# Value products of two key tiles in one run, every second slot, with four tiles of exponentials

## The chip, the cores and the metric

One core of a Trainium2 chip. The metric is device time in microseconds (us) of one launch. The engines have these names: PE is TensorE's matmuls, PEld its weight loads, DVE is VectorE, ACT is ScalarE, POOL is GpSimd, SP is SyncE, which issues the DMAs.

## What is computed

Two layers over a stream `x` of 8 batches x 100 tokens x 128. Each layer adds a gated cross-attention to a context of 1444 keys per batch, then a gated mixture of experts:

```
x = x + tanh(g_xattn[l]) * attention_l(layernorm(x), context)
x = x + tanh(g_ffn[l])   * experts_l(layernorm(x))
```

Attention has 16 heads of 8. Layer 0 masks keys; layer 1 multiplies the attention weights of each key with a sigmoid of its "energies". Layer 0's experts choose 8 of 64 by groups, layer 1's 2 of 8. Only the attention part is touched by the change, in both layers.

## The kernel before

Everything is written as one program for each engine, and the engines are tied by semaphores alone. The order on an engine is the order in the code.

**Tiling.** The 1444 keys of a batch are cut into 12 key tiles of 121 rows (the last has 113). The 16 heads are four groups (g = 0 to 3) of four heads; one score matmul gives a group's scores of a key tile: 121 keys x 400 (4 heads x 100 queries). The scores land in `ps`, which has two PSUM banks, used in turn. ACT takes each bank through the exponential into `probs` (L847), one instruction per group. `weigh` (L1177 to L1193) then multiplies the exponentials of a whole key tile with the values, 16 small matmuls that the trace shows as 32 records on PE (32 columns of weights each), accumulating in the bank `po`.

**Slots.** A batch is 12 slots, one for each key tile t (L1232 to L1253). The PE's order in a slot is written out by hand. In what follows s0 to s3 are the score matmuls of the four groups, each in layer 0 with a mask matmul behind it (L1167, L1171), W is one `weigh` run, and Q ("quad") is four matmuls into `pm` (L1137) with which the row maxima of a later batch are found:

- layer 0: s0, s1, Q, W, s2, s3, then `beside`
- layer 1: s0, s1, W, s2, Q, s3, then `beside`

W in slot t is that of the tile before, t-1 (in slot 0 the last tile of the batch before). `beside` (L1215) puts other work behind s3: the turning and projection of the batch before in slots 1 to 3, the key projections of a later batch in slots 4 to 6 (L1102), the value projections of the next one in slots 7 to 9 (L1115). Batch 7, the last, has no Q, nor have the last two slots of batch 6.

**Waits.** A score matmul n waits until ACT has emptied its bank, which is exponential n-2 (L1165). The exponential waits for its scores and, as `probs` has two tiles, for W of the tile two before (L846). W waits for all four exponentials of its tile (L1179). Q goes in two halves of two banks each; its first half waits for the first half of the quad before to be taken by DVE, its second half for the second (L1133 to L1136). In layer 0 a quad's kind is "pair" (DVE L423, two instructions) or "third" (L427, four); each third quad is a third. In layer 1 it is two reductions (L420).

**ACT's order** in a slot: exponentials 0, 1, (the copy of `po` of the batch before in slot 0), 2, 3, and behind them in slots 4 to 6 the copy of the key projection (L857), in slots 7 to 9 that of the value projection (L871).

**Others that wait for W.** SP stacks the keys of batch b (L1393) and POOL makes its queries and values (L694, L706) when all W of batch b-2 are done.

**Buffers.** `wb` (four tiles of 128 x 800) holds routing weights during the experts' stage alone.

Of the kernel before, what the change touches and what calls it, by code (L numbers as in the profile page):

```python
# [32 lines left out]
ACT = mybir.ActivationFunctionType  # L33
AX = mybir.AxisListType.X

B, S, D = 8, 100, 128
NK = 1444
KEY_TILE = 121
KEY_TILES = -(-NK // KEY_TILE)
# [3 lines left out]
HQ = H * S  # L43
GQ = J * S
# [6 lines left out]
TOK = B * S  # L51
# [13 lines left out]
RING = 4  # L65
# [28 lines left out]


MASK_ROWS = 31


PARTS = {"a": (0, 6), "b": (6, 8)}
# [29 lines left out]
def flamingo(nc, a, out, scratch):  # L129
    with ExitStack() as ctx:  # L130
        def sb(name, shape, dt=F32):
            return ctx.enter_context(nc.sbuf_tensor(name, shape, dt))
# [66 lines left out]
        rowmax = sb("rowmax", [100, 128])  # L199
        mrow = sb("mrow", [H, S], F32R)  # L200
        junk = sb("junk", [100, 2, 2, MAX_W], BF16)
        probs = [sb(f"probs{i}", [KEY_TILE, HQ]) for i in range(2)]
        oraw = sb("oraw", [128, GQ])
        rden = sb("rden", [100, H])
        onorm = sb("onorm", [100, D])
# [20 lines left out]
            return v  # L226

        wts = [sb(f"wts{i}", [128, 3, 128]) for i in range(RING)]
        wb = [sb(f"wb{i}", [128, TOK]) for i in range(RING)]
        sg = [over(tmpf, v * HALF, [128, HALF]) for v in range(2)]  # L230
        tu = [over(vaug[0], TOK + v * HALF, [128, HALF]) for v in range(2)]
        hw = [over(tmpf, 2 * HALF, [128, HALF]), over(t2, 0, [128, HALF])]
# [556 lines left out]
        def _(act):  # L789
            n = [0]  # L790
# [47 lines left out]
            def attention(l):  # L838
                s = A[l]

                def exp_group(b, t, g):
                    r, n = rows_of(t), (b * KEY_TILES + t) * G + g
                    act.wait_ge(s["scores_ready"], n + 1)

                    if b * KEY_TILES + t >= 2:
                        act.wait_ge(s["pv_done"], b * KEY_TILES + (t - 1))  # L846
                    nc.scalar.activation(probs[t % 2][0:r, g * GQ:(g + 1) * GQ], ps[0:r, n % 2, 0:GQ], ACT.Exp,  # L847
                                         scale=SCALE).then_inc(s["probs_ready"], 1)

                def k_high(b, c):  # L850
                    lo, w = CHUNKS[c]
                    act.wait_ge(s["kproj_done"], b * 3 + (c + 1))
                    if b >= 2 and c == 0:

                        act.wait_ge(s["chunk_ready"], (b - 1) * 2 * QUADS)
                        act.wait_ge(s["kstack_in"][b % 2], landed(b - 2, b % 2, 2, 192))
                    nc.scalar.activation(khi[b % 2][:, lo:lo + w], pc[:, 0:w], ACT.Identity, bias=bk[l][:, 0:1])\  # L857
                        .then_inc(s["khi_ready"], 1)

                def max_row(b):  # L860

                    act.wait_ge(s["maxrow_ready"], b + 1)
                    if b >= 1:
                        act.wait_ge(s["mrow_in"][(b - 1) % 2], landed(b - 1, (b - 1) % 2, 2, 16))
                    nc.scalar.activation(mrow[:], pc[0:H, 0:S], ACT.Identity, scale=-1.0).then_inc(s["mrow_ready"], 1)

                def v_raw(b, c):
                    act.wait_ge(s["vproj_done"], b * 3 + (c + 1))

                    act.wait_ge(s["v_written"], (b * 3 + c - 1) * (1, 2)[l])  # L870
                    nc.scalar.copy(vraw[(c + b) % 2][:].rearrange("p t n -> p (t n)"), pc[0:KEY_TILE, :])\  # L871
                        .then_inc(s["vraw_ready"], 1)

                def outputs(b):

                    act.wait_ge(s["pv_done"], b * KEY_TILES + KEY_TILES)
                    if b >= 1:
                        act.wait_ge(s["onorm_ready"], b)
                    nc.scalar.copy(oraw[:], po[:, 0:GQ]).then_inc(s["oraw_ready"], 1)

                def slots(b):

                    for t in range(KEY_TILES):
                        exp_group(b, t, 0)
                        exp_group(b, t, 1)
                        if b >= 1 and t == 0:
                            outputs(b - 1)
                        exp_group(b, t, 2)
                        if t == ROW_SLOT and b < B - 1:
                            max_row(b + 1)  # L890
                        exp_group(b, t, 3)
                        if b < B - 2 and 0 <= t - K_SLOT < 3:
                            k_high(b + 2, t - K_SLOT)
                        if b < B - 1 and 0 <= t - V_SLOT < V_CHUNKS:
                            v_raw(b + 1, t - V_SLOT)
                        if b == B - 1:

                            if t == 0:
                                root(2 * l + 1, "a")
                            if t == TURN_SLOT:  # L900
                                part_turned(2 * l + 1, 0)
                                part_turned(2 * l + 1, 1)
                            if t == LOGITS_SLOT and l == 0:
                                router0("a")

                for c in range(len(CHUNKS)):
                    k_high(1, c)
                max_row(0)
                slots(0)
                if l == 0:  # L910
                    act.wait_ge(dve_done, marks["energy"])
                    step(nc.scalar.activation(egate[:], egate[:], ACT.Exp, scale=-1.0), "energy_exp")
                for b in range(1, B):
                    slots(b)
                outputs(B - 1)
# [112 lines left out]
        def _(pe):  # L1028
            n = [0]
# [58 lines left out]
            def attention(l):  # L1088
                s = A[l]
# [87 lines left out]
                def weigh(b, t):  # L1177
                    r = rows_of(t)
                    pe.wait_ge(s["probs_ready"], (b * KEY_TILES + t) * G + G)  # L1179
                    if t == 0:  # L1180

                        pe.wait_ge(s["v_written"], (b * 3 + 3) * (1, 2)[l])
                        if b >= 1:
                            pe.wait_ge(s["oraw_ready"], b)
                    for g in range(G):
                        for j in range(J):
                            h = J * g + j
                            mm = nc.tensor.matmul(po[32 * j:32 * j + 32, g * S:(g + 1) * S],  # L1188
                                                  vaug[b % 2][0:r, t, 9 * h:9 * h + 32],
                                                  probs[t % 2][0:r, h * S:(h + 1) * S],  # L1190
                                                  start=(t == 0 and g == 0), stop=(t == KEY_TILES - 1),
                                                  tile_position=(0, 32 * j), skip_group_check=True)
                    mm.then_inc(s["pv_done"], 1)  # L1193
# [38 lines left out]
                def slots(b):  # L1232

                    for t in range(KEY_TILES):
                        if t < ROW_SLOT:
                            quad = (b + 1, QUADS_AHEAD + t) if b < B - 1 else None
                        else:
                            quad = (b + 2, t - ROW_SLOT) if b < B - 2 else None
                        scores(b, t, 0)
                        scores(b, t, 1)  # L1240
                        if quad and l == 0:
                            max_quad(*quad)
                        if t >= 1:
                            weigh(b, t - 1)
                        elif b >= 1:
                            weigh(b - 1, KEY_TILES - 1)
                        scores(b, t, 2)
                        if t == ROW_SLOT and b < B - 1:
                            max_rows(b + 1)
                        if quad and l == 1:  # L1250
                            max_quad(*quad)
                        scores(b, t, 3)
                        beside(b, t)  # L1253
# [7 lines left out]
                    max_quad(1, k)  # L1261
                for b in range(B):
                    slots(b)
                weigh(B - 1, KEY_TILES - 1)
                turn_out(B - 1)
                turn_back(B - 1)
# [109 lines left out]
        def _(sp):  # L1376
# [93 lines left out]
            def experts(l):  # L1470
# [10 lines left out]
                def spread(u, slot):  # L1481

                    if not (isinstance(u, int) and u < RING):

                        sp.wait_ge(m["weighted"], u * 2 - (2 * RING - 2))
                    if l == 0:
                        for i in range(2):
                            sp.dma_start(wb[slot][64 * i:64 * i + 64, :],
                                         scratch[0][bass.ds(u * 2 + i, 1), :].broadcast_to([64, TOK]))\
                                .then_inc(m["wb_in"][slot], 16)  # L1490
                    else:
                        sp.dma_start(wb[slot][:], scratch[1][bass.ds(u * 16, 16), :].unsqueeze(1)
                                     .broadcast_to([16, 8, TOK])).then_inc(m["wb_in"][slot], 16)

                for u in range(RING):
# [98 lines left out]
```

## Time and profile before

| | us |
|---|---|
| median of 3 runs | 1073.51 |
| lowest, highest | 1071.07, 1082.74 |
| profiled execution, first to last instruction (span) | 1069.7 |
| PE busy | 912.3 |
| DVE busy | 749.6 |
| ACT busy | 579.7 |

No time of the profiled execution besides its span is listed; what lies around the span is read from the runs: the lowest is 1.4 above it, the median 3.8. In the rows below a timeline line reads: start, duration (us), engine, line of the code, operation, output <- input, shape, count; in brackets the idle time of that engine just before, and what ended it. Matmul ends are modelled, so starts are the safer reading; the start of a weight load (PEld) is where a matmul enters PE.

### The profile page before, as it was taken

The page shows a single profiled execution, that of the slowest core. Times are in us where ns is not written, and L with a number is a line of the kernel's source. Part 1 is how long each engine was busy: PE and PEld are TensorE (multiplying, and loading weights), DVE is VectorE, ACT ScalarE, POOL GpSimd, SP SyncE. Part 2 cuts the span into 40 slices and gives each one's busy share as a digit, 9 for nine tenths or more (in the row PEclk, how much of TensorE's full clock was granted, in tenths as well). Part 3 has the DMA queues.
Part 4 walks back from the last instruction along what each step waited for, and adds up shares of the span by engine and source line. Part 5 has one row for each costly group of instructions (what it writes and reads, how often), then busy time and mean ns, then how long its engine had stood idle before and what let it go on. Part 6 is the DMA issues. An engine that isn't in the chain of part 4 may idle for free.

```text
span 1069.7 us, 24592 instructions
## 1 busy us (share of the span) xinstructions
PE 912.3 (85%) x9812; PEld 631.5 (59%) x9812; DVE 749.6 (70%) x1420; ACT 579.7 (54%) x1214; POOL 309.6 (29%) x276
## 2 busy tenths in 40 slices
PE   4569899999999987699997679999999998842996
PEld 2126566666666654588885236566666656532885
DVE  6676677777676727589997966877877874042996
ACT  2305465665655575256664135777767767621664
POOL 2600202112112100167673501242234212002764
PEclk9558899999999998599998657999999998865999
DMA  6670404034032110376551620431342231016651
GB/s 152 113 160 2 101 13 113 30 85 112 30 85 47 40 32 2 89 213 170 163 152 25 159 58 1 113 95 48 86 112 57 58 85 32 1 18 133 166 160 54
DMA packets 49007, 90.01 MB, mean 84 GB/s; under 512 B 21816, under 2 KB 32252, under 8 KB 48892
## 3 DMA queue, kind: packets, MB, share of 16 engines
q1 hardware_dynamic: 48892, 88.44, 34.4%
q8 instruction: 77, 1.26, 0.5%
q14 instruction: 38, 0.31, 0.1%
HBM read 47.32 MB, written 1.75 MB: 46 GB/s over the span
## 4 chain that ended last, share of the span: by engine, by line
PE 59%; DVE 14%; ACT 9%; POOL 6%; issue 5%; DMA 4%; SPq 2%; POOLq 0%; DVEq 0%; ACTq 0%
PE ps L1167 20%; PE po L1188 15%; PE pm L1137 9%; POOL tmpf L771 6%; ACT probs L847 4%; PE ps L1171 4%; PE pc L1102 4%; PE pc L1115 3%; DVE vaug L533 3%; DVE qsel L524 3%; ACT qsel L941 3%; DMA routing<-vaug 2%; DVE mx_part L420 2%; DVE junk L423 2%; DVE junk L427 1%
## 5 line engine op out<-in xcount | busy, mean ns | idle before, releaser
L847 ACT ACTIVATE probs<-ps 121x400 f32<-121x400 f32 (+1 forms) x768 | 356.8, 503 | 211.7 <-PE ps L1171 126.0
L1167 PE MATMUL ps<-qst,kst 128*121 128x400 f32 (+3 forms) x768 | 318.9, 461 | 30.1 <-ACT probs L847 29.0
L420 DVE TENSOR_REDUCE mx_part<-pm 100x2 f32<-100x964 f32 x192 | 213.7, 1158 | 65.6 <-PE pm L1137 65.5
L1167 PEld LDWEIGHTS ps<-qst,kst 128*121 128x121 f32 (+3 forms) x768 | 141.9, 189 | 146.4 <-ACT probs L847 91.3
L1276 PE MATMUL pm<-qsel,qst 128*128 128x400 f32 x660 | 158.3, 363 | 39.8 <-DVE qsel L524 35.9
L423 DVE CUSTOM_DVE_ANT_0 junk<-pm,negq 100x964 bf16<-100x964 f32 x128 | 143.5, 1158 | 55.6 <-PE pm L1137 55.5
L1188 PE MATMUL po<-probs,vaug 121*32 121x100 f32 x6144 | 179.3, 259 | 1.5 <-ACT probs L847 1.5
L1188 PEld LDWEIGHTS po<-probs,vaug 121*32 121x32 f32 x6144 | 135.2, 113 | 55.1 <-ACT probs L847 32.0
L1137 PE MATMUL pm<-khi,qbd 32*100 32x482 f32 x768 | 129.5, 490 | 37.4 <-DVE mx_part L420 12.9
L1276 PEld LDWEIGHTS pm<-qsel,qst 128*128 128x128 f32 x660 | 122.2, 195 | 58.8 <-DVE qsel L524 57.9
L771 POOL TENSOR_TENSOR tmpf<-vaug,wb 128x400 f32<-128x400 f32 x55 | 68.4, 1243 | 220.3 <-DMA wb<-routing 160.6
L1171 PE MATMUL ps<-negT,ident_b 121*121 121x276 bf16 (+1 forms) x384 | 111.5, 290 | 0.0
L1137 PEld LDWEIGHTS pm<-khi,qbd 32*100 32x100 f32 x768 | 46.8, 174 | 104.0 <-issue 34.7
L524 DVE TENSOR_TENSOR qsel<-tmpf,qsel 128x400 fp32r<-128x400 f32 x55 | 61.9, 1126 | 49.2 <-ACT qsel L941 49.2
L712 POOL TENSOR_TENSOR vaug<-vraw,bv 121x512 f32<-121x512 f32 x24 | 31.8, 1327 | 220.6 <-ACT vraw L871 212.0
L427 DVE CUSTOM_DVE_ANT_0 junk<-pm,negq 100x482 bf16<-100x482 f32 x128 | 76.6, 655 | 21.9 <-PE pm L1137 21.9
L1276 PE MATMUL ps<-qsel,qst 128*128 128x400 f32 x330 | 83.3, 363 | 1.1 <-DVE qst L516 1.1
L712 POOL TENSOR_TENSOR vraw<-vraw,bv 121x512 f32<-121x512 f32 x24 | 30.7, 1277 | 173.4 <-ACT vraw L871 173.4
L941 ACT CAST qsel<-tmpf 128x400 fp32r<-128x400 f32 x55 | 29.0, 527 | 88.0 <-POOL tmpf L771 88.0
L696 POOL TENSOR_TENSOR qst<-qsel,head_mask 96x400 fp32r<-96x400 f32 x64 | 52.6, 851 | 76.6 <-PE po L1188 67.9
L771 POOL TENSOR_TENSOR t<-vaug,wb 128x400 f32<-128x400 f32 x55 | 73.0, 1327 | 0.0
L1276 PEld LDWEIGHTS ps<-qsel,qst 128*128 128x128 f32 x330 | 64.4, 200 | 1.7 <-DVE qsel L568 1.4
(179 smaller groups left out, 893.3 us busy)
## 6 DMA issues: line engine op xcount, KB each, us to landing
kst<-khi SPq DMA_DIRECT2D x128, 180.5 KB, 4.0
wb<-routing SPq DMA_DIRECT2D x66, 200.0 KB, 3.7
ctxT<-in_ctxT SPq DMA_DIRECT2D x16, 722.0 KB, 4.2
kst<-klo SPq DMA_DIRECT2D x64, 180.5 KB, 4.0
wts<-in_experts SPq DMA_DIRECT2D x55, 192.0 KB, 3.7
wb<-routing SPq DMA_DIRECT2D x22, 400.0 KB, 4.1
qsel<-qhi SPq DMA_DIRECT2D x16, 100.0 KB, 2.4
kst<-kst SPq DMA_DIRECT2D x7, 180.5 KB, 3.4
```

What stands on the lines that cost most here:

```text
L420: ins = nc.vector.tensor_reduce(parts[:, 2 * i:2 * i + 2, j, x], bank, AX, ALU.max)
L423: ins = nc.vector.tensor_tensor_reduce(junk[:, i], bank, mask, 1.0, -3e38, ALU.add, ALU.max, parts[:, x + i, j, 0:1])
L427: ins = nc.vector.tensor_tensor_reduce(junk[:, i, g % 2, :], pm[0:S, g, 0:MAX_W], negq[:, NK - MAX_W:NK], 1.0, -3e38, ALU.add, ALU.max, pa ...
L524: nc.vector.tensor_tensor(h_lo[v], hw[v], h_hi[v], ALU.subtract).then_inc(m["h_low"], 1)
L712: nc.gpsimd.tensor_tensor(raw4 if l else dst, raw4, bias, ALU.add).then_inc(s["v_written"], 1)
L771: nc.gpsimd.tensor_tensor(hw[v], tu[v], wb[slot][:, v * HALF:(v + 1) * HALF], ALU.mult).then_inc(m["weighted"], 1)
L847: nc.scalar.activation(probs[t % 2][0:r, g * GQ:(g + 1) * GQ], ps[0:r, n % 2, 0:GQ], ACT.Exp, scale=SCALE).then_inc(s["probs_ready"], 1)
L1137: mm = nc.tensor.matmul(pm[0:S, bank, 0:MAX_W], qbd[b % 2][rows, j * S:(j + 1) * S], khi[b % 2][rows, lo:lo + MAX_W], start=True, stop=Tru ...
L1167: mm = nc.tensor.matmul(ps[0:r, n % 2, 0:GQ], kst[b % 2][0:rows, g, t * KEY_TILE:t * KEY_TILE + r], qst[b % 2][0:rows, g * GQ:(g + 1) * GQ ...
L1171: mm = nc.tensor.matmul(ps[0:r, n % 2, 0:GQ].rearrange("p (j q) -> p j q", q=S)[:, :, MASK_ROWS:S], ident_b[0:r, 0:r], negT[0:r, t, MASK_R ...
L1188: mm = nc.tensor.matmul(po[32 * j:32 * j + 32, g * S:(g + 1) * S], vaug[b % 2][0:r, t, 9 * h:9 * h + 32], probs[t % 2][0:r, h * S:(h + 1) ...
L1276: mm = nc.tensor.matmul(dst, w, x, start=(alone and k == 0), stop=(alone and k == 2), skip_group_check=not alone)
```

## The change

`probs` becomes a ring of four tiles; the two new tiles lie over the memory of `wb`, which becomes one tensor, `shared`. The exponential of tile t waits for W of tile t-4. In odd slots there is no W. In even slots t there are two W, of tiles t-2 and t-1, one behind the other at the place where one stood (in slot 0 those of the last two tiles of the batch before). Behind the last slot of batch 7 stand two W. The number of matmuls, exponentials and transfers stays as it was.

```diff
+PROBS = 4
...
-        probs = [sb(f"probs{i}", [KEY_TILE, HQ]) for i in range(2)]
...
-        wb = [sb(f"wb{i}", [128, TOK]) for i in range(RING)]
+        shared = sb("shared", [128, RING * TOK])
+        wb = [shared[:, i * TOK:(i + 1) * TOK] for i in range(RING)]
+        probs = [sb(f"probs{i}", [KEY_TILE, HQ]) for i in range(2)] + [over(shared, i * HQ, [KEY_TILE, HQ]) for i in range(2)]
...
-                    if b * KEY_TILES + t >= 2:
-                        act.wait_ge(s["pv_done"], b * KEY_TILES + (t - 1))
-                    nc.scalar.activation(probs[t % 2][0:r, g * GQ:(g + 1) * GQ], ps[0:r, n % 2, 0:GQ], ACT.Exp,
+                    if b * KEY_TILES + t >= PROBS:
+                        act.wait_ge(s["pv_done"], b * KEY_TILES + (t - PROBS + 1))
+                    nc.scalar.activation(probs[t % PROBS][0:r, g * GQ:(g + 1) * GQ], ps[0:r, n % 2, 0:GQ], ACT.Exp,
...
-                                                  probs[t % 2][0:r, h * S:(h + 1) * S],
+                                                  probs[t % PROBS][0:r, h * S:(h + 1) * S],
...
-                        if t >= 1:
+                        if t >= 1 and t % 2 == 0:
+                            weigh(b, t - 2)
                             weigh(b, t - 1)
-                        elif b >= 1:
+                        elif t == 0 and b >= 1:
+                            weigh(b - 1, KEY_TILES - 2)
                             weigh(b - 1, KEY_TILES - 1)
...
+                weigh(B - 1, KEY_TILES - 2)
                 weigh(B - 1, KEY_TILES - 1)
...
-                        sp.dma_start(wb[slot][:], scratch[1][bass.ds(u * 16, 16), :].unsqueeze(1)
+                        sp.dma_start(wb[slot], scratch[1][bass.ds(u * 16, 16), :].unsqueeze(1)
```

## Rows read from the trace of the kernel before

**Rows 1.** The page: busy time by engine, and the chain's shares.
```profile
PE 912.3 (85%) x9812; PEld 631.5 (59%) x9812; DVE 749.6 (70%) x1420; ACT 579.7 (54%) x1214; POOL 309.6 (29%) x276
...
PE 59%; DVE 14%; ACT 9%; POOL 6%; issue 5%; DMA 4%; SPq 2%; POOLq 0%; DVEq 0%; ACTq 0%
```

**Rows 2.** Stretches of 50 us, layer 1: busy time by engine, granted clock.
```profile
core 0: us, PE busy (x) PEld busy (x) DVE busy (x) ACT busy (x) POOL busy (x), PEclk, DMA share, GB/s
...
600.00:650.00 50.00, 39.17 (x223) 17.74 (x225) 35.84 (x36) 13.12 (x26) 7.38 (x9) 0.50 0.30 68
...
750.00:800.00 50.00, 47.79 (x691) 30.19 (x691) 39.53 (x45) 35.04 (x74) 15.13 (x16) 1.00 0.47 105
```

**Rows 3.** Timeline, layer 0, batch 3: slot 1's s2 up to slot 2's s2.
```profile
216.84 0.18 PEld L1167 LDWEIGHTS ps<-qst,kst 128*121 128x121 f32 x1 [0.15 <-issue]
...
218.00 0.18 PEld L1167 LDWEIGHTS ps<-qst,kst 128*121 128x121 f32 x1
...
218.29 0.08 DVE L423 DVE_READ_ACCUMULATOR2_ANT mx_part<- 100x1 f32 x1
...
218.39 0.18 PEld L1167 LDWEIGHTS ps<-qst,kst 128*121 128x121 f32 x1 [0.16 <-ACT probs L847]
...
218.60 0.90 ACT L847 ACTIVATE probs<-ps 121x400 f32<-121x400 f32 x2 [0.26 <-PE ps L1171]
...
218.89 0.25 PEld L1137 LDWEIGHTS pm<-khi,qbd 32*100 32x100 f32 x4 [0.27 <-issue]
...
219.50 0.67 PEld L1188 LDWEIGHTS po<-probs,vaug 121*32 121x32 f32 x32 [0.36 <-ACT probs L847]
...
220.32 0.18 PEld L1167 LDWEIGHTS ps<-qst,kst 128*121 128x121 f32 x1 [0.15 <-issue]
```

**Rows 4.** Timeline, same batch: DVE's end of a quad, and the next quad.
```profile
225.20 0.08 DVE L427 DVE_READ_ACCUMULATOR2_ANT mx_part<- 100x1 f32 x1
...
225.65 0.68 PE L1137 MATMUL pm<-khi,qbd 32*100 32x482 f32 x4
...
232.29 0.08 DVE L423 DVE_READ_ACCUMULATOR2_ANT mx_part<- 100x1 f32 x1
...
232.95 0.47 PE L1137 MATMUL pm<-khi,qbd 32*100 32x482 f32 x4
```

**Rows 5.** Timeline, layer 1, a batch's slot 0 from s2 to slot 1's quad.
```profile
749.79 0.18 PEld L1167 LDWEIGHTS ps<-qst,kst 97*121 97x121 f32 x1 [0.15 <-ACT probs L847]
...
750.16 0.17 PEld L1137 LDWEIGHTS pm<-khi,qbd 32*100 32x100 f32 x4 [0.19 <-DVE mx_part L420]
...
750.66 2.23 DVE L420 TENSOR_REDUCE mx_part<-pm 100x2 f32<-100x964 f32 x2 [0.76 <-PE pm L1137]
751.03 1.54 ACT L847 ACTIVATE probs<-ps 121x400 f32<-121x400 f32 x3 [0.21 <-PE ps L1167]
...
751.58 0.18 PEld L1167 LDWEIGHTS ps<-qst,kst 97*121 97x121 f32 x1 [0.53 <-ACT probs L847]
...
751.96 0.67 PEld L1188 LDWEIGHTS po<-probs,vaug 121*32 121x32 f32 x32 [0.20 <-ACT probs L847]
...
752.78 0.18 PEld L1167 LDWEIGHTS ps<-qst,kst 97*121 97x121 f32 x1 [0.15 <-ACT probs L847]
...
753.15 0.17 PEld L1137 LDWEIGHTS pm<-khi,qbd 32*100 32x100 f32 x4 [0.19 <-issue]
```

**Rows 6.** Timeline, layer 1, slot 5, behind a key projection: exponentials, then s2.
```profile
764.42 1.53 ACT L847 ACTIVATE probs<-ps 121x400 f32<-121x400 f32 x3
...
764.96 0.44 PE L1167 MATMUL ps<-qst,kst 97*121 97x400 f32 x1
```

**Rows 7.** Timeline, layer 1, batch 7: s0 and s1 of a slot, then s2 and s3.
```profile
925.94 0.84 PE L1167 MATMUL ps<-qst,kst 97*121 97x400 f32 x2 [0.41 <-ACT probs L847]
...
927.53 0.63 PE L1167 MATMUL ps<-qst,kst 97*121 97x400 f32 x2
```

**Rows 8.** The chain in order of time, layer 1, batch 0: W of two slots.
```profile
634.90 1.49 PE po L1188 x32
639.57 1.49 PE po L1188 x32
```

## The prediction

> **What bounds the kernel now.** I read the page first. PE is busy for 85% of the span and carries 59% of the chain that ended last; DVE and ACT have 14% and 9% [rows 1]. That asks for less PE time, and the change seems to give it, since two W in one run enter and leave W's form of matmul once. But a busy share is an average. So I went on to the timeline of one slot in each layer, for which wait ends last at each step.
>
> Layer 0 [rows 3]: from s2 (216.84) to the next slot's s1 (218.39) are 1.55 us in which s1 waits for ACT. From s1 to the quad 0.50, quad to W 0.61, W to s2 0.82: PE alone. Together 3.48, the slot. Layer 1 [rows 5]: s2 (749.79) to s1 (751.58) 1.79, again ended by ACT; s1 to W 0.38, W to s2 0.82; together 2.99. So the stretch from s1 to s2, where W stands, is PE's, and while W runs ACT makes exponentials 0 and 1, for which s2 and s3 must wait. The reader is to see that W covers ACT's latency, and that DVE's quad ends only shortly before the next quad begins (218.29 + 0.08 = 218.37 against 218.89 [rows 3]).
>
> **The change part by part.**
>
> *Counts.* Each layer has 96 W. 48 leave odd slots. 47 come as the second run in an even slot (slots 2 to 10 of eight batches are 40, slot 0 of batches 1 to 7 are 7), and one more stands behind the last slot, where PE waits for exponentials anyway: I count it as nothing (0.67 at most).
>
> *The second run.* No row shows two W in a row. One W's 32 weight loads take 0.67, and s2 starts 0.15 behind the last [rows 3, 5]. A second W of the same form should add 0.67; at most 0.82, if the way out is paid again; a gain is excluded, as 32 pairs of instructions must be issued. I take 0.67, since inside W the 32 follow without a gap: 47 x 0.67 = 31.5 us per layer.
>
> *Odd slots, layer 0.* Without W, s2 follows the quad. Rows show quad to W at 0.61; quad to s2 I take as the same, as both change the form of the matmul. So 0.82 goes, if s2's bank is free: exponential 0 starts 0.60 behind s0 and lasts some 0.45 (two take 0.90), to 219.05; s2 would enter at 219.50. It is free. I take 0.81 a slot. What is late next is DVE. The next quad comes 0.81 earlier, and its second half needs the whole quad before. From slot 1: DVE done 218.37, some 0.04 to PE, quad due at 218.89 - 0.81 = 218.08: a stall of 0.33 [rows 3]. Behind a third quad: 225.28 + 0.04 against 225.65 - 0.81, 0.48; behind the extra DVE work and the longer slots 5 to 9: 232.37 + 0.04 against 232.95 - 0.81, 0.27 [rows 4]. With slots 1 and 11 at 0.33, slot 3 at 0.48, slots 5, 7, 9 at 0.27 it is 1.95 a batch, bounds 0 and 6 x 0.48 = 2.9. Even slots have their long run behind the quad, so DVE catches up there.
> Layer 0: six odd slots save 4.9 in each of batches 0 to 6, 34; batch 7 has no quad, s2 waits for exponential 0 and saves about 0.6 (end 219.05, so 0.70 behind s1 in place of 0.50 + 0.82 [rows 3]), 3.6; stalls are 6 x 1.95 and about 1.5 in batch 6, 13.2. So 31.5 + 13.2 - 37.6 = +7.
>
> *Odd slots, layer 1.* Here W stands straight between s1 and s2, and ACT decides once it is gone. Exponentials 3, 0, 1 start at 751.03 and run on (pitch about 0.46, one 0.50 long); exponential 0 ends at 751.99, so s2 can enter at 752.04 instead of 752.78: 0.74 saved [rows 5]. But the quad behind s2 moves to 752.41, and DVE finishes the quad before at 750.66 + 2.23 = 752.89; with 0.04 the second half is released 0.52 late. 0.22 is left. In slots 5, 7 and 9 ACT first copies a projection: exponential 0 runs from 764.42 to 764.92 and s2 enters at 764.96 already now [rows 6]: nothing is saved there, and W in these slots was free. So slots 1, 3, 11 give 0.22 each, 0.66 a batch, 4.0 in batches 0 to 5; batch 6 (no key projections, no quad in its last slots) 1.6; batch 7: s0 at 925.94, exponential 0 ends 0.47 + 0.50 later, s2 enters near 926.95 instead of 927.53 [rows 7], 0.58 x 6 = 3.5. Layer 1: 31.5 - 9.1 = +22. Bounds: 0.74 saved in all 21 odd slots of batches 0 to 6 that have no copy and no stall (about 11 us less) and nothing saved anywhere (9 us more).
>
> *Ring, waits, buffers.* The exponential's wait is now for W of tile t-4, which has run at least a slot earlier: it never ends last, but it also brings no earlier start, since `ps` still has two banks and an exponential needs its scores. Behind the wait in ACT's queue stand only later exponentials. SP's key stacks and POOL's queries and values for the next batch come free 0.67 later, in slot 0, and are due a batch later (some 35 us): nothing. SP issues the same transfers into the same bytes of `wb` in the experts' stage, when no exponential is live: nothing.
>
> *The clock.* In 600 to 650 us PE was granted 0.50, its 1.2 GHz, and a slot of layer 1 took 4.67 us (634.90 to 639.57) [rows 2, 8]; at 1.00 it takes 2.99. If the rise comes a slot earlier or later through the new rhythm, that is 1.7 us each time. I take 0, with 8 either way (five slots).
>
> *Sum:* 7 + 22 = +29 on the span of 1069.7, so 1098.7. The runs lie 1.4 (lowest) to 3.8 (median) above the span; I add 2: 1101 us, against the median of 1073.5.
>
> *A rule weighed.* Rows show gaps of 0.15 behind W and 0.20 before it in layer 1 [rows 5]. The Trainium skill, "TensorEngine Tiling (Array Packing)", Key Properties, states that a change of tiling mode drains TensorE. The trace agrees as far as there is a gap at each such change; by the rule alone each joined pair of runs would save PE these gaps, which is the first rival below.
>
> **The rivals.**
>
> *PE alone decides (faster).* If s2 didn't wait for ACT nor the quad for DVE, an odd slot would save 0.81 in layer 0, and in layer 1 1.20 less the 0.37 between s2 and the quad, 0.83 [rows 5]; less 0.67 that is 0.14 and 0.16 a pair, 47 x 0.30 = 14: 1058 us. For it: PE's share. Against it: both layers' s1 already wait for ACT, and two banks leave ACT no lead. It decides if exponential 0 ended before s1 + 0.37 in layer 1; the rows have 0.41 without the quad's wait, so it would also need DVE's quad 0.5 us shorter.
>
> *DVE doesn't stall (within 1%).* If the quad's second half has its banks in time, 13 go in layer 0 and about 11 in layer 1: +5, 1077 us. For it: matmul ends and releases are inferred. Against it: quad and DVE starts are measured, and 2.23 + 0.50 exceeds 752.41 - 750.16.
>
> *The second run pays its entry again (slower still).* 94 x 0.15 = 14 more: 1115 us.
>
> *The clock.* If batch 0 of layer 1 stays at 1.2 GHz, or batch 7 falls lower for longer, up to 8 more: 1109 us; sooner up: 1093.
>
> **How the numbers follow.** The forecast 0.62 (its own range 1090 to 1109, with the clock at its bounds), PE alone 0.10, no stall 0.15, entry paid again 0.08, more clock loss 0.05. A measurement of this kernel tells about 1% (10.7 us) from no change. Faster by over 1%: the first rival, 0.10. Within 1%: the second, and a tail of the forecast, 0.17. Slower: 0.73. The range of 1076 to 1113 leaves out the first rival and half of the third, and holds the bounds of the unknown costs but for their extremes.
>
> **What would show it.** Right: in the new timeline W comes as a run of 64 with weight loads of about 1.34 us; odd slots of layer 1 about 2.8 us with s2 ended by ACT and the quad by DVE, even ones about 3.7; odd slots of layer 0 about 2.7, even ones about 4.4 with the quad ended by DVE; PE's idle time before L1167 and L1137 grown, its busy time about as before. Wrong: odd slots in layer 1 near 2.1 us; a quad that never waits for DVE; or more than 0.1 us between the two runs.

## The result, and the profile after

The changed kernel takes 1140.57 us (median of 4 runs, 1135.45 to 1144.25) against 1072.29 for the kernel before (4 runs beside it, 1068.88 to 1082.74): a ratio on record of 1.0595, with an interval of 1.0515 to 1.0676; the two medians alone give 1.0637, so a difference between runs that is given in us is good to some 5 us. The sign was as forecast, the size was not: 1101 was predicted, and 1113 was the upper end. The profiled execution took 1141.88 us, its span is 1140.1.

Line numbers in the new kernel are 4 higher up to W (L1141 is the quad, L1171 the scores, L1192 W, L851 the exponential). The two new tiles of exponentials appear as `shared`. First the page of the changed kernel, the rows that answer to [rows 1], with the granted clock in 40 slices:

```profile
PE 962.0 (84%) x9812; PEld 672.2 (59%) x9812; DVE 749.1 (66%) x1420; ACT 578.1 (51%) x1214; POOL 309.8 (27%) x276
...
PEclk9559899999999996799996598986868988775999
...
PE 55%; DVE 18%; ACT 9%; issue 6%; POOL 5%; DMA 4%; SPq 2%; POOLq 0%; ACTq 0%; DVEq 0%
```

The clock line of the kernel before, from its page:

```profile
PEclk9558899999999998599998657999999998865999
```

PE does the same 9812 instructions and is busy 50 us longer. DVE's share of the chain grew from 14% to 18%, as a quad that waits for DVE would have it. But the largest difference is in the clock line. Before, after the dip of layer 1's first batch (6, 5, 7), there are eight slices at 9. After, the dip (6, 5) is followed by 9, 8, 9, 8, 6, 8, 6, 8, 9, 8, 8. The next view says it in numbers; it is that of 50 us stretches of the changed kernel (columns as in [rows 2]):

```profile
750.00:800.00 50.00, 45.46 (x527) 29.84 (x527) 31.34 (x35) 28.20 (x61) 11.06 (x11) 0.80 0.26 61
800.00:850.00 50.00, 46.46 (x521) 30.18 (x519) 30.32 (x34) 26.61 (x57) 11.05 (x11) 0.73 0.26 61
```

In the middle of layer 1 the granted clock is 0.80 and 0.73, where it was 1.00 [rows 2], and PE gets through 527 matmuls in 50 us instead of 691. PE's busy share hardly shows it (45.46 against 47.79 us), since the same matmuls are busy for longer at 1.2 GHz (W's run of 64 further down: 1.36 us of weight loads at 2.4 GHz, 2.54 at 1.2).

To see where the time went I take the length of each batch, from one copy of `po` (ACT, slot 0) to the next, in the timelines:

| us a batch | layer 0, batches 1 to 7 | sum | layer 1, batches 1 to 7 | sum |
|---|---|---|---|---|
| before | 46.3, 42.3 x4, 40.2, 37.9 | 293.7 | 37.2 x5, 36.0, 37.7 | 259.6 |
| after | 47.9, 43.5 x4, 41.2, 39.8 | 302.9 | 44.9, 45.1, 47.8, 50.0, 44.9, 44.2, 41.2 | 318.0 |

The copies that bound a batch of layer 1, before and after (in the changed kernel the longest batch):

```profile
712.71 0.49 ACT L879 COPY oraw<-po 128x400 f32<-128x400 f32 x1 [0.35 <-PE po L1188]
749.92 0.49 ACT L879 COPY oraw<-po 128x400 f32<-128x400 f32 x1 [0.35 <-PE po L1188]
```

```profile
825.00 0.49 ACT L883 COPY oraw<-po 128x400 f32<-128x400 f32 x1 [2.35 <-PE po L1192]
875.01 0.49 ACT L883 COPY oraw<-po 128x400 f32<-128x400 f32 x1 [2.25 <-PE po L1192]
```

Layer 0 grew evenly, by 1.2 in each of its batches 2 to 5 and 9.2 in all. Layer 1 grew by 58.4, and unevenly, though its batches 1 to 5 do identical work: that is no sum of waits, which would be the same in each.

**Layer 0** in the timeline of the changed kernel, an odd slot's s1 up to the next slot's s2, answers to [rows 3]:

```profile
219.83 0.18 PEld L1171 LDWEIGHTS ps<-qst,kst 128*121 128x121 f32 x1 [0.16 <-ACT probs L851]
...
220.33 0.25 PEld L1141 LDWEIGHTS pm<-khi,qbd 32*100 32x100 f32 x4 [0.26 <-issue]
220.95 0.18 PEld L1171 LDWEIGHTS ps<-qst,kst 128*121 128x121 f32 x1 [0.37 <-ACT probs L851]
...
222.50 0.18 PEld L1171 LDWEIGHTS ps<-qst,kst 128*121 128x121 f32 x1 [0.16 <-ACT probs L851]
...
223.00 0.16 PEld L1141 LDWEIGHTS pm<-khi,qbd 32*100 32x100 f32 x1 [0.27 <-issue]
223.34 0.25 PEld L1141 LDWEIGHTS pm<-khi,qbd 32*100 32x100 f32 x3 [0.18 <-DVE mx_part L427]
223.95 1.36 PEld L1192 LDWEIGHTS po<-probs,vaug 121*32 121x32 f32 x64 [0.36 <-ACT shared L851]
225.46 0.18 PEld L1171 LDWEIGHTS ps<-qst,kst 128*121 128x121 f32 x1 [0.15 <-issue]
```

The odd slot is 222.50 - 219.83 = 2.67 long (2.7 was forecast). In the even one W comes as one run of 64, 1.36 of weight loads, and W to s2 is 1.51 where it was 0.82: a second W costs 0.69. The quad waits for DVE: W enters 0.95 behind the quad's first load (223.00 to 223.95), 0.34 later than the 0.61 of before. A pair of slots thus pays 0.69 + 0.34 - 0.81 = 0.22, six pairs 1.3 a batch.

**Layer 1** in the same view, slots 0 to 2 of batch 1, answers to [rows 5]:

```profile
685.59 1.36 PEld L1192 LDWEIGHTS po<-shared,vaug 121*32 121x32 f32 x64 [0.19 <-ACT probs L851]
687.10 0.18 PEld L1171 LDWEIGHTS ps<-qst,kst 97*121 97x121 f32 x1 [0.15 <-issue]
...
688.90 0.18 PEld L1171 LDWEIGHTS ps<-qst,kst 97*121 97x121 f32 x1 [0.53 <-ACT probs L851]
689.30 0.18 PEld L1171 LDWEIGHTS ps<-qst,kst 97*121 97x121 f32 x1 [0.21 <-ACT probs L851]
689.67 0.16 PEld L1141 LDWEIGHTS pm<-khi,qbd 32*100 32x100 f32 x2 [0.19 <-issue]
690.26 0.17 PEld L1141 LDWEIGHTS pm<-khi,qbd 32*100 32x100 f32 x2 [0.43 <-DVE mx_part L424]
...
692.99 2.54 PEld L1192 LDWEIGHTS po<-probs,vaug 121*32 121x32 f32 x64 [0.47 <-issue]
```

Up to 690.26 every step is as forecast: s2 to s1 1.80 as before, s1 to s2 0.40 (forecast 0.46), and the quad's second half comes 0.59 behind its first, released by DVE (forecast 0.52). Then the next run of W takes 2.54 for the same 64 loads. The windows of 1 us at this place, same columns, show why:

```profile
689.00:690.00 1.00, 1.00 (x4) 0.43 (x4) 1.00 (x2) 0.86 (x3) 1.00 (x2) 1.00 0.91 205
690.00:691.00 1.00, 0.86 (x5) 0.33 (x3) 1.00 (x2) 0.28 (x1) 1.00 (x2) 0.68 0.96 208
691.00:692.00 1.00, 1.00 (x5) 0.86 (x6) 1.00 (x2) 0.43 (x1) 0.38 (x1) 0.50 0.94 191
```

The clock fell from 2.4 to 1.2 GHz (0.50) at about 690.4 (the microsecond from 690 has 0.68), in the slot that no longer has a W. Read in fine windows, batches 1 to 6 of layer 1 hold 13 such falls with some 92 us at 1.2 GHz in all; the kernel before has none in these batches. The ten of batches 1 to 5 all begin behind the W of slot 10 and ahead of that of slot 4, and end before the W of slot 6; from slot 4 to slot 9, where `beside` has the key and value projections, none begins. The three of batch 6, which has no key projections, come in slots 3 to 7. Each of the 13 begins between two runs of W. At 1.2 GHz a run of 64 to s2 takes 2.82 (692.99 to 695.81) instead of 1.51.

The waits of the changed kernel, engine, line, what it waited for, then total, times, longest:

```profile
DVE mx_part L424 <- PE pm L1141: 118.4, 68, 4.4
...
PEld pm L1141 <- DVE mx_part L424: 32.2, 38, 3.3
```

and of the kernel before:

```profile
DVE mx_part L420 <- PE pm L1137: 65.5, 86, 2.4
...
PEld pm L1137 <- DVE mx_part L420: 28.8, 39, 3.3
```

DVE waits 53 us more for layer 1's quads. So DVE is not what holds layer 1: over most of a batch it is PE, which is slow, that is late.

### The profile page after: what moved, and what is told of

Same layout as the page of the kernel before. It is cut to its first block, busy times and chain, and to the rows that moved or that the text cites. A ratio compares the mean times of both kernels' runs of the same rounds, so it can differ in the third digit from the quotient of the medians.

```text
span 1140.1 us, 24576 instructions
## 1 busy us (share of the span) xinstructions
PE 962.0 (84%) x9812; PEld 672.2 (59%) x9812; DVE 749.1 (66%) x1420; ACT 578.1 (51%) x1214; POOL 309.8 (27%) x276
## 4 chain that ended last, share of the span: by engine, by line
PE 55%; DVE 18%; ACT 9%; issue 6%; POOL 5%; DMA 4%; SPq 2%; POOLq 0%; ACTq 0%; DVEq 0%
PE ps L1171 16%; PE po L1192 15%; PE pm L1141 9%; DVE mx_part L424 5%; POOL tmpf L775 5%; PE pc L1106 4%; PE ps L1175 3%; PE pc L1119 3%; DVE qsel L528 2%; DVE vaug L537 2%; ACT shared L851 2%; ACT qsel L945 2%; DVE junk L431 2%; ACT probs L851 2%; DMA routing<-vaug 2%
## 5 line engine op out<-in xcount | busy, mean ns | idle before, releaser
L1171 PE MATMUL ps<-qst,kst 128*121 128x400 f32 (+3 forms) x768 | 330.6, 476 | 48.0 <-ACT probs L851 25.0
L1171 PEld LDWEIGHTS ps<-qst,kst 128*121 128x121 f32 (+3 forms) x768 | 147.2, 197 | 185.2 <-ACT probs L851 69.3
L851 ACT ACTIVATE shared<-ps 121x400 f32<-121x400 f32 (+1 forms) x384 | 177.7, 502 | 136.0 <-PE ps L1175 66.1
L851 ACT ACTIVATE probs<-ps 121x400 f32<-121x400 f32 x384 | 178.7, 504 | 126.3 <-PE ps L1175 61.9
L1141 PE MATMUL pm<-khi,qbd 32*100 32x482 f32 x768 | 152.5, 511 | 40.8 <-DVE mx_part L424 14.2
L775 POOL TENSOR_TENSOR tmpf<-vaug,shared 128x400 f32<-128x400 f32 x55 | 68.5, 1245 | 228.9 <-DMA shared<-routing 167.1
L1141 PEld LDWEIGHTS pm<-khi,qbd 32*100 32x100 f32 x768 | 56.2, 179 | 119.9 <-issue 44.1
L1192 PE MATMUL po<-shared,vaug 121*32 121x100 f32 (+1 forms) x3072 | 91.1, 280 | 0.0
L1192 PE MATMUL po<-probs,vaug 121*32 121x100 f32 x3072 | 88.3, 275 | 0.0
L1192 PEld LDWEIGHTS po<-shared,vaug 121*32 121x32 f32 (+1 forms) x3072 | 79.4, 125 | 14.4 <-issue 8.1
L1192 PEld LDWEIGHTS po<-probs,vaug 121*32 121x32 f32 x3072 | 77.0, 123 | 15.5 <-issue 8.0
```

What stands on the lines that cost most here:

```text
L775: nc.gpsimd.tensor_tensor(hw[v], tu[v], wb[slot][:, v * HALF:(v + 1) * HALF], ALU.mult).then_inc(m["weighted"], 1)
L851: nc.scalar.activation(probs[t % PROBS][0:r, g * GQ:(g + 1) * GQ], ps[0:r, n % 2, 0:GQ], ACT.Exp, scale=SCALE).then_inc(s["probs_ready"], 1)
L1141: mm = nc.tensor.matmul(pm[0:S, bank, 0:MAX_W], qbd[b % 2][rows, j * S:(j + 1) * S], khi[b % 2][rows, lo:lo + MAX_W], start=True, stop=Tru ...
L1171: mm = nc.tensor.matmul(ps[0:r, n % 2, 0:GQ], kst[b % 2][0:rows, g, t * KEY_TILE:t * KEY_TILE + r], qst[b % 2][0:rows, g * GQ:(g + 1) * GQ ...
```

## The experiments

Two theories of the falls stood against each other. A: the odd slots have lost work and gained waits (for ACT behind s1, for DVE in the quad), and PE, so thinned, falls in clock; the expectations below name the waits alone. R: the run of 64 small matmuls does it by itself. All ratios are against the kernel before on the same chip.

**The ring alone (ring_only).** The order of before, with four tiles of exponentials in the new places:

```diff
-if t >= 1 and t % 2 == 0:
-    weigh(b, t - 2)
+if t >= 1:
     weigh(b, t - 1)
-elif t == 0 and b >= 1:
-    weigh(b - 1, KEY_TILES - 2)
+elif b >= 1:
     weigh(b - 1, KEY_TILES - 1)
...
-weigh(B - 1, KEY_TILES - 2)
```

> The ring of four tiles and the shared memory, with one W in each slot as before. Both theories: the ring's wait never ends last and the place of the tiles costs nothing, so the time of before, 1072 us within 5, low clock in layer 1 only in batches 0 and 7. If the place of the two new tiles or the wait costs something, it shows here as more than 5 us.

1069.23 us, ratio 0.9969 (0.9941 to 0.9997). The ring, its waits and the shared memory cost nothing, and bring next to nothing. Layer 1 ran at full clock:

```profile
750.00:800.00 50.00, 47.80 (x710) 30.24 (x702) 39.87 (x45) 34.75 (x74) 15.16 (x16) 1.00 0.47 105
```

**Pairs in one layer (pairs_l0, pairs_l1).** The order of after where `l == 0` (or `l == 1`), that of before in the other layer:

```diff
-if t >= 1 and t % 2 == 0:
-    weigh(b, t - 2)
-    weigh(b, t - 1)
+if l == 0:
+    if t >= 1 and t % 2 == 0:
+        weigh(b, t - 2)
+        weigh(b, t - 1)
...
+elif t >= 1:
+    weigh(b, t - 1)
```

> Two W in even slots in layer 0 alone, single W in layer 1. Forecast by the prediction's sum for layer 0: 7 us more than before, 1079 us; layer 1 as before, with its clock at 2.4 GHz in batches 1 to 6. If the loss were spread evenly over the layers it would be 1106 us.

1080.24 us, ratio 1.0062 (1.0036 to 1.0087): 6.7 us, as forecast. Its layer 0 took 300.9 in seven batches, 7.2 over before; its layer 1 the 259.6 of before.

> Two W in even slots in layer 1 alone, single W in layer 0. If layer 1 holds 22 us of waits and some 35 us of low clock: 1130 us, with stretches of 1.2 GHz in batches 1 to 6. If layer 0 holds half of the loss: 1106 us.

1137.13 us, ratio 1.0565 (1.0488 to 1.0642). By the ratios some 61 of the changed kernel's 64 us are layer 1's (by the medians 63 of 68), 7 more than expected, and they come without the other layer's change:

```profile
800.00:850.00 50.00, 45.46 (x529) 29.70 (x527) 30.81 (x34) 28.13 (x60) 12.28 (x12) 0.80 0.26 61
```

**The quad later (late_quad).** The changed kernel, with layer 1's quad behind s3 in odd slots, so that it comes later and waits less for DVE:

```diff
-if quad and l == 1:
+if quad and l == 1 and t % 2 == 0:
     max_quad(*quad)
 scores(b, t, 3)
+if quad and l == 1 and t % 2 == 1:
+    max_quad(*quad)
```

> The changed kernel with the quad of layer 1's odd slots behind s3, so that DVE has some 0.6 us more to finish the quad before. Theory A (the waits in the odd slots leave PE so idle that its clock falls): the wait for DVE goes, some 10 us, and the clock falls in fewer stretches: 1095 to 1115 us. Theory R (the run of 64 small matmuls itself lets the clock fall, the waits don't matter for it): the 10 us go but the low stretches stay: 1125 to 1132 us.

1111.67 us, ratio 1.0356 (1.0301 to 1.0411), with the same runs of 64. Batches 1 to 5 of layer 1 are 41.0 to 41.9 long where they were 44.9 to 50.0, and little more than one fall of 3.4 us a batch is left in them; batch 6 has several and is 43.0 long.

```profile
750.00:800.00 50.00, 45.41 (x672) 30.13 (x673) 35.78 (x39) 31.94 (x69) 16.43 (x16) 0.97 0.27 63
```

That is on A's side. PE's busy time is that of the changed kernel (45.41 against 45.46), with 672 matmuls in place of 527: a busy share does not tell the two apart.

**Half the products (half_products).** The changed kernel without the second W: the products of even key tiles are left out, so even slots have one run of 32 and odd slots none (the semaphore counts are adapted).

```diff
...
 if t >= 1 and t % 2 == 0:
-    weigh(b, t - 2)
     weigh(b, t - 1)
 elif t == 0 and b >= 1:
-    weigh(b - 1, KEY_TILES - 2)
     weigh(b - 1, KEY_TILES - 1)
...
-weigh(B - 1, KEY_TILES - 2)
```

> The changed order with only the second W of each pair: odd slots have none, even slots one, so no run of 64 is left; the products of the even key tiles are left out. The waits in the odd slots stay. By the prediction's sum layer 0 loses 24 us and layer 1 9 us against the kernel before. Theory A (the waits let the clock fall): stretches of 1.2 GHz in layer 1's batches 1 to 6 as in the changed kernel, some 30 us: 1060 to 1075 us. Theory R (the runs of 64 let it fall): no such stretches, 1035 to 1045 us.

1093.61 us, ratio 1.0201 (1.0135 to 1.0268). With 96 W less this kernel is slower than the one before. Both missed the size (A said 1060 to 1075, R 1035 to 1045), but R failed: no run of 64 is left, and the clock was low for longer than in the changed kernel.

```profile
750.00:800.00 50.00, 45.89 (x385) 27.78 (x384) 35.36 (x41) 31.20 (x66) 12.19 (x13) 0.77 0.42 96
```

Layer 0, which keeps its clock, gained: 39.4 a batch against 42.3. Layer 1 lost, 40.5 to 51.9 a batch against 37.2. The same saving makes the one layer faster and the other slower, since in layer 1 the clock falls.

**Each W twice (each_twice).** The kernel before, with every W run a second time in its own slot (numerator and denominator both double):

```diff
-for g in range(G):
+for again, g in [(k, g) for k in range(2) for g in range(G)]:
...
-    start=(t == 0 and g == 0), stop=(t == KEY_TILES - 1),
+    start=(t == 0 and g == 0 and again == 0), stop=(t == KEY_TILES - 1 and again == 1),
```

> The kernel before with each W issued twice in its slot (numerator and denominator are both doubled): a run of 64 in every slot of both layers and no odd slot without W. 192 second runs of 0.69 us: 132 us. Theory A: no new waits, the clock stays at 2.4 GHz in layer 1's batches 1 to 6, 1200 to 1210 us. Theory R: the clock falls in most slots of layer 1, over 1235 us.

1185.02 us (a single run; 1069.98 for the kernel before), 15 under A's range and 50 under R's bound. This is a run of 64 in every slot, and from 702.6 to behind the last batch the clock stays up. The window of 50 us, one run in the timeline, and the page's clock line:

```profile
750.00:800.00 50.00, 48.56 (x1017) 34.40 (x1020) 33.03 (x37) 29.15 (x62) 11.07 (x11) 1.00 0.27 62
```

```profile
704.60 1.36 PEld L1188 LDWEIGHTS po<-probs,vaug 121*32 121x32 f32 x64 [0.19 <-ACT probs L847]
```

```profile
PEclk8559999999999999689998569999999999985899
```

Runs of 64 do not bring the clock down by themselves: R failed a second time. A batch grew by 8.3 in layer 0 (42.3 to 50.6) and 8.2 in layer 1 (37.2 to 45.4), 12 times 0.69: the price of a second run, with no other wait in it. A's range was 15 too high: it charged all 192 runs in full, but batch 7 of layer 1, for one, grew by 3.4 alone (41.1 against 37.7), as it has none of the 13.7 us at 1.2 GHz that the kernel before has there.

**Idle matmuls in odd slots (filled, filled_three).** The changed kernel, with two matmuls of zeros added to `po` before s2 and again before the quad, in odd slots of layer 1:

```diff
+def filler(b, t):
...
+    for k in range(2):
+        nc.tensor.matmul(po[:, 0:GQ], zero_b[:, 0:128], zero_b[:, 0:GQ], start=False, stop=False,
+                         skip_group_check=True)
...
+if l == 1 and t % 2 == 1:
+    filler(b, t)
...
 scores(b, t, 2)
...
 if quad and l == 1:
+    if t % 2 == 1:
+        filler(b, t)
     max_quad(*quad)
```

> The changed kernel with idle work on PE in layer 1's odd slots: two matmuls of zeros (128 x 400, added to the accumulators) ahead of s2 and two ahead of the quad, where PE waits for ACT and for DVE anyway. The waits end when they did. Theory A: PE's clock stays at 2.4 GHz in batches 1 to 6, some 30 us go: 1100 to 1112 us. Theory R: the low stretches stay, 1130 to 1145 us.

1106.54 us, ratio 1.0334 (1.0263 to 1.0405), in A's range. PE does more work and the kernel is 34 us faster than the changed one: no fall in batches 1 to 6 (in the page's clock line, behind the dip of batch 0 stand ten slices at 9).

```profile
750.00:800.00 50.00, 47.05 (x649) 29.97 (x649) 34.69 (x37) 32.10 (x68) 14.60 (x14) 1.00 0.26 61
```

```profile
PEclk9558899999999988599998579999999999875999
```

Batches 1 to 5 are 41.8 long, 4.6 over before, where 3.4 was forecast. In slots 5, 7 and 9 the idle matmuls stand in PE's way (the runs of W in slots 6 and 8 are 7.42 apart, 7.06 in the changed kernel), so the next kernel has them in slots 1, 3 and 11 alone.

```diff
-if t > 1 or b >= 1:
+if (t > 1 or b >= 1) and t in (1, 3, 11):
```

> As the filled kernel, but with the idle matmuls in slots 1, 3 and 11 alone, where PE waits for ACT and DVE; in slots 5, 7 and 9 of the filled kernel the two ahead of the quad stood in no wait and cost 0.36 us each. Theory A: the clock stays at 2.4 GHz in batches 1 to 6 and what is left is the prediction's sum without the clock, 1.1 us a batch of layer 1 less than the filled kernel: 1097 to 1101 us. If the projections' slots needed the idle work too, low stretches come back: over 1106 us.

1104.05 us, ratio 1.0297 (1.0247 to 1.0348), 3 over what was expected. Batches 1 to 5 are 40.7 long, without a fall: 3.5 over before. The runs of W in slots 0, 2 and 4 of a batch stand 6.47 and 6.48 apart:

```profile
680.71 1.36 PEld L1192 LDWEIGHTS po<-shared,vaug 121*32 121x32 f32 x64 [0.20 <-ACT probs L851]
687.18 1.36 PEld L1192 LDWEIGHTS po<-probs,vaug 121*32 121x32 f32 x64 [0.20 <-issue]
693.66 1.36 PEld L1192 LDWEIGHTS po<-shared,vaug 121*32 121x32 f32 x64 [0.19 <-ACT probs L851]
```

Two slots of before are 2 x 2.99 = 5.98, so a pair costs 0.49; 0.67 - 0.22 = 0.45 was forecast. More than the 3 us are in batches 6 and 7 (42.1 and 42.4), where the clock falls from 904.3 on; `filled`, with idle matmuls in all odd slots, has 39.0 and 38.6 there.

**Both remedies (late_filled).** The later quad, with idle matmuls before s2 and before s3 in odd slots of layer 1:

```diff
+if l == 1 and t % 2 == 1:
+    filler(b, t)
 scores(b, t, 2)
...
-if quad and l == 1:
+if quad and l == 1 and t % 2 == 0:
     max_quad(*quad)
+if l == 1 and t % 2 == 1:
+    filler(b, t)
 scores(b, t, 3)
+if quad and l == 1 and t % 2 == 1:
+    max_quad(*quad)
```

> Late quad and idle matmuls together: the changed kernel with layer 1's odd quads behind s3, two matmuls of zeros ahead of s2 and two ahead of s3 in odd slots. Theory A: no wait for DVE and no low clock in batches 1 to 6. What is left is the second W (31 us a layer) against what odd slots save with ACT alone as their limit: layer 0's 7 us and in layer 1 31.5 less about 20, so 1085 to 1098 us. If the odd slots of layer 1 were held by something else than DVE and ACT, no gain over the two single edits: 1105 us or more.

1093.25 us, ratio 1.0218 (1.0184 to 1.0252), in the range of A. In odd slots the quad is no longer split by a wait, its four weight loads come together, and the clock holds in batches 1 to 6:

```profile
689.95 0.17 PEld L1141 LDWEIGHTS pm<-khi,qbd 32*100 32x100 f32 x4 [0.24 <-DVE mx_part L424]
```

```profile
750.00:800.00 50.00, 46.71 (x656) 29.55 (x659) 35.84 (x39) 33.46 (x72) 15.69 (x15) 1.00 0.31 76
```

It is the best version with pairs in both layers that was tried, and it is still slower than the kernel before: batches 1 to 5 of layer 1 take 40.1 to 40.4 against 37.2, idle matmuls included. With the 7.2 that pairs_l0 loses in layer 0, this shows that the pairs lose without the clock too.

**Idle matmuls in the kernel before (warm).** Its clock is low in batch 0 of layer 1 [rows 2, 8]. In both layers, matmuls of zeros were put behind the quads that open the attention (3 behind each of batch 0's, 8 behind each of batch 1's), and 8 behind W in slot 1 of batch 7, into banks that are written anew afterwards:

```diff
+def warm(bank, count):
+    for k in range(count):
+        nc.tensor.matmul(bank, zero_b[:, 0:128], zero_b[:, 0:512], start=True, stop=True,
+                         skip_group_check=True)
...
...
 max_quad(0, k)
+warm(ps[:, 0, :], 3)
...
```

> The kernel before with idle matmuls (zeros, into banks that are free then) where PE waits long: three behind each opening quad, eight behind each of the last two, eight in batch 7 where ACT loads its tables. If the low clock in batch 0 and batch 7 comes from those waits, batch 0 of layer 1 saves some 11 us, layer 0 some 3, batch 7 some 4: 1052 to 1062 us. If it has another cause: 1070 to 1080 us.

1060.49 us, ratio 0.9896 (0.9842 to 0.9949): in the range of the first case, and faster than both kernels by work that computes nothing. Batch 7 of layer 1 is 34.6 long where it was 37.7. The stretch that [rows 2] shows at 0.50 is at 0.90:

```profile
600.00:650.00 50.00, 43.11 (x343) 19.14 (x341) 40.68 (x40) 17.29 (x34) 7.38 (x9) 0.90 0.29 67
```

## Why the prediction was right or wrong, point by point

*The second run, 0.67.* Right: 0.69 in both layers, and no entry is paid again; that rival fell. The rule that was weighed is worth little here: in layer 0 a pair saves PE 0.81 in the odd slot and costs 0.69 in the even one, so the joined run spares 0.12, near the gap of 0.15 behind W, and DVE's stall of 0.34 takes more than that.

*Layer 0, +7.* Right: 7.2 in pairs_l0, 9.2 in the profile of the changed kernel (in batches 2 to 5 both have 43.5 a batch; they differ in batches 1 and 7). The odd slot and DVE's stall came out to within 0.03.

*Layer 1's waits, 4.02 - 0.66, about 3.4 a batch.* Right: 3.5 in batches 1 to 5 of filled_three, which keep the clock. Slots 5, 7 and 9 saved nothing, as said: the runs of slots 6 and 8 are 671.89 - 664.83 = 7.06 apart at full clock, and before the change the W of these slots stood 773.69 - 767.29 = 6.40 apart; the difference, 0.66, is the second W alone. The rows, changed kernel and kernel before:

```profile
664.83 1.36 PEld L1192 LDWEIGHTS po<-probs,vaug 121*32 121x32 f32 x64 [0.27 <-issue]
671.89 1.36 PEld L1192 LDWEIGHTS po<-shared,vaug 121*32 121x32 f32 x64 [0.26 <-issue]
```

```profile
767.29 0.67 PEld L1188 LDWEIGHTS po<-probs,vaug 121*32 121x32 f32 x32 [0.27 <-issue]
773.69 0.67 PEld L1188 LDWEIGHTS po<-probs,vaug 121*32 121x32 f32 x32 [0.27 <-issue]
```

The sum of these terms (1101) is near filled_three (1104). That it comes so near in all is in part luck: the falls of batches 6 and 7 add some 7 us to filled_three (against `filled`), and the dip in its batch 0, shorter than that of the kernel before (below), takes some off.

*The rivals on the faster side.* "PE alone" needed odd slots of layer 1 without waits; the rows above show both. "DVE doesn't stall" is refuted by the quad rows of both layers.

*The clock.* This is the step that failed: "I take 0, with 8 either way (five slots)". It cost some 32 to 36 us: the changed kernel and filled_three differ by idle matmuls alone, by 36.5 in the medians (1140.57 and 1104.05) and by 0.030 in the ratios (1.0595 and 1.0297), which is 32. Batches 1 to 5 of layer 1 hold 232.6 - 203.5 = 29.1 of it, for some 78 us at 1.2 GHz. The two profiles are 4.9 apart at slot 0 of batch 1 already (its W at 685.59 against 680.71), but 2.3 of that stand at the layer's first W (647.23 against 644.93), ahead of the first idle matmul, where the two programs are still the same; the other 2.6 lie in batch 0, whose dip ends at 659.6 in the one and at 648.3 in the other. Measured against the kernel before, the change did not prolong that dip: its last stretch at 1.2 GHz is 61.4 long before (594.5 to 656.0), 51.2 after (608.4 to 659.6) and 44.4 in filled_three. The forecast, and its rival "the clock" as well, asked only how long the dips that were already there would last. It did not ask whether an odd slot without W would make new ones. Of the signs that the prediction named for its being right, one failed with it: PE's busy time, "about as before", rose by 49.7. The trace of before had a hint, though not a clean one: its second dip, 901.7 to 915.4, lies in batch 7, the only batch with neither quads nor projections, where a slot holds least for PE. But it begins in the one long wait of that batch, 2.29 us in which ACT loads tables, and `warm`, with idle matmuls in that wait, has 3.4 us at 1.2 GHz in batch 7 instead of 13.7:

```profile
902.19 0.67 PEld L1167 LDWEIGHTS ps<-qst,kst 97*121 97x121 f32 x2 [2.29 <-ACT probs L847]
```

*What brings it down* is shown as far as this. Batches 1 to 6 of layer 1 hold 0 us at 1.2 GHz in the kernel before and some 92 in the changed one. Taking W out of a slot and leaving it out altogether (half_products) brings more, some 149; making the quad wait less (late_quad) brings less, some 34; idle matmuls in all odd slots bring it to 0 (filled, late_filled), in slots 1, 3 and 11 to some 10, all in batch 6 (filled_three); a W more in every slot, none taken out, has 0 (each_twice). What the runs do not separate is how much of it is missing work and how much waiting, as an emptied slot has both. The Trainium skill, "TensorE: Matmul & The Clock Gate", "A second HAM failure mode: psum-queue depth-cycling", tells of a kernel whose TensorE idles so often for short moments between groups of matmuls that its clock swings between the two levels. The trace agrees as far as the clock swings 13 times, with gaps of 0.19 to 0.53 in the rows of layer 1 above; but gaps of that size stand in [rows 5] too, where no fall came. Taken as a rival, this rule would have moved the forecast the right way. Why filled_three falls again in batches 6 and 7 stays open, and so does a kernel with `warm` and pairs together, which was not tried.

## What to carry to other kernels

Before work is taken out of a stretch in which TensorE is held up by other engines, ask whether that work was what kept its clock up; a forecast at the old clock is only good if the granted clock stays, and a dip elsewhere in the same trace is a reason to doubt that it does. Work that stands between two dependent steps may be free where it is, because it covers another engine's latency: here W covered ACT's exponentials and DVE's quads, and moving it cost its full 0.69 in one slot and saved 0.47 (layer 0), or in layer 1 0.20 at most and nothing beside the projections, in the other. Where the clock does fall, matmuls on zeros placed in the waits are a cheap test, and at times the remedy.

## What the runs showed of the hardware

The clock fell to 1.2 GHz at a place where the view of windows has PE busy for 1.00 and 0.86 of the two microseconds around it, and no long wait stands ahead of any of the 13 falls: PE's longest idle time in the 10 us before them is 0.30 to 0.72 us, and the kernel before has up to 0.58 in the same batches without a fall. The granted clock has to be read for itself. A few idle matmuls in slots 1, 3 and 11 took some 32 to 36 us off a kernel of 1140 us, and others, at the head of each layer's attention and in a wait of batch 7, took 1.0% off the kernel before. Removing 96 of 192 runs of W made a kernel 2.0% slower than the one that has them all. The 64 small matmuls of a double run follow one another without any seam: 1.36 us of weight loads at 2.4 GHz, 2.54 at 1.2.
